# VectorE's loop begun in the middle of a half, and TensorE's 64-row and 64-column products put side by side, in the two local-attention layers of a fused kernel

## The chip, the cores and the metric

One core of one Trainium2 chip runs the whole program in one launch. The metric is the device time of that launch in microseconds, the median of three runs. A profiled execution of the same program gives the trace. Its engines are TensorE (PE, with its weight loads shown as PEld), VectorE (DVE), ScalarE (ACT), GpSimd (POOL) and SyncE (SP, which issues the DMAs).

## What is computed

The program is an RWKV-like block (stages "setup", "mix", "scan", "gate") followed by two layers of windowed attention with a gated MLP (stages "local0", "local1"). The change touches the two local layers alone. For a sequence of 4096 tokens, a batch of 2, 256 channels and 8 heads of 64, each layer computes, all in fp32:

```
h = shift_token(x); q, k, v = split(h @ wqkv)
q = l2norm(q) * qs; k = l2norm(k) * ksc; q, k = rotary_xpos(q, k)
sim = (8 q) @ [k_before, k_own]^T        # a window of 128 queries sees its own and the earlier 128 keys
attn = softmax(mask(sim)); o = attn @ [v_before, v_own]
x = x + o @ wo
h = layernorm(shift_token(x)) * lg + lb
a, g = split(h @ w1 + b1)
x = x + (a * gelu(g)) @ w2 + b2
```

## The kernel before

`local_stage` (line 1409) runs one layer. The tokens of each of the two sequences ("streams" s = 0 and 1) are cut into NW = 32 windows u of 128 tokens. The unit of work is a half, `half(s, u, w)`: the attention of window u of stream s, and, between its pieces, two things for the other stream o: the MLP of its last attended window, and the projection, norm and rotation of q, k and v of its next window. So a layer is 64 halves that alternate between the streams. w is the parity of the window, which picks the buffer.

Every engine has its own written-out order in its own `half`, and semaphores tie them together (`S`, `Q`, `M`, `E` hold them; `.after(n)` is the count to wait for). There is no scheduler. The helper `run` (line 1469) gives all engines the same loop: the first half is written out, then a hardware loop `Fori` of 15 turns with four halves each, then the last halves written out:

```
def body(i, more):
    half(1, 2 * i, 0)
    half(0, 2 * i + 1, 1, more=more)
    half(1, 2 * i + 1, 1, more=more)
    if more:
        half(0, 2 * i + 2, 0)
```

So on every engine the loop's branch stands between the end of one half and the start of the next one.

TensorE's half (line 2106). A half has four head pairs hp. `scores` (line 1997) of one pair are two products of 64 contracted rows, one in the upper and one in the lower 64 rows of the array, into two banks; the profile shows them as `64*128 64x256`, at line 2010. `values` (line 2027) of one pair are products with 64 output columns, `128*64 128x128`, at line 2033. All others use the array whole (`128*128`): `mean` and `variance` of the layer norm (lines 2047, 2053), `project` (line 1976: q, k, v for j = 0, 1, 2), `turn` (line 2024: transposes of the probabilities of a pair), `hidden` (line 2070: three groups of w1), `out` (line 2078: three groups of w2), `turn_q`, `turn_k` (lines 1985, 1993), `project_out` (line 2041), and in layer 1 `turn_out` (line 2086). An fp32 product is executed in two passes, so a `project` is four records, a `hidden` sixteen.

VectorE's half (line 1787). `row_max` (line 1686) adds the mask to the scores of a pair and takes the row maximum (`l_pause` at line 1695 is its first instruction, line 1697 its two main ones, line 1704 the scaled negative maximum `nb`). `inverse_sums` (line 1684) inverts the row sums of a pair. `rotate_q` (lines 1647 to 1649), `sum_q`, `sum_k`, `clamp`, `add_q`, `norm_k` prepare the other stream's q and k. `evacuate` (line 1717) copies the turned probabilities of pairs 1 and 3 to SBUF; ScalarE does pairs 0 and 2. `gate` (line 1751) multiplies the MLP's two halves, one call for each of three groups. `head_out` (line 1711) copies a pair's value product out. `carry` (lines 1725, 1729) copies the last token to the next window and, where w is 0, sets a mask. `attended` (line 1735) adds the residual.

Who waits for whom around the change: `scores` of pair 2 and 3 wait for `row_max` of pair 0 and 1, whose banks they take; `hidden` of group 0 waits for `hn`, which GpSimd makes (line 1591) in its queue behind `normalise` of pair 1 (line 1584), which waits for VectorE's `inverse_sums` of pair 1; `hidden` of group 1 waits for `norm_k`; `out` of group j waits for `gate` of group j; `values` of pair 2 and 3 wait for `head_out` of pair 0 and 1 and for the two `evacuate`s.

Of the kernel before, what the change touches and what calls it, by code (L numbers as in the profile page):

```python
# [1408 lines left out]
def local_stage(nc, persist, a, T, layer):  # L1409
# [5 lines left out]
    NW = T // P  # L1415
    NHP = HEADS // 2
    LAST = layer == 1
# [3 lines left out]
    with ExitStack() as ctx:  # L1421
# [73 lines left out]
        with nc.Block() as block:  # L1495
# [141 lines left out]
            def _(dve):  # L1637
# [69 lines left out]
                def head_out(s, u, hp):  # L1707

                    dve.wait_ge(Q["pv"][s].sem, Q["pv"][s].after(u * NHP + hp))
                    dve.wait_ge(S["wo_ps"][s].sem, S["wo_ps"][s].after(u, 1))  # L1710
                    nc.vector.tensor_copy(oT[s][:, hp], bank[s][OUT[hp % 2]][:, 0:P]).then_inc(Q["oT"][s].sem, 1)
# [72 lines left out]
                    add_q(0, 0)  # L1784
                    norm_k(0, 0)

                def half(s, u, w, mlp=True, more=True):
                    o = 1 - s
                    (um, wm_), (un, wn) = partner(s, u, w)
                    after = s == 0 or more  # L1790
                    row_max(s, u, w, 0)
                    if mlp:
                        deviate(o, um, wm_)
                    row_max(s, u, w, 1)
                    inverse_sums(s, u, 0)
                    if after:
                        rotate_q(o, un, wn)
                    row_max(s, u, w, 2)
                    inverse_sums(s, u, 1)
                    if after:  # L1800
                        sum_q(o, un)
                    row_max(s, u, w, 3)
                    inverse_sums(s, u, 2)
                    if after:
                        sum_k(o, un)
                        clamp(o, un)
                        add_q(o, un)
                    inverse_sums(s, u, 3)
                    if after:
                        norm_k(o, un)  # L1810
                    evacuate(s, u, 1)
                    if mlp:
                        gate(o, um, 0)
                    head_out(s, u, 0)
                    if mlp:
                        gate(o, um, 1)
                    head_out(s, u, 1)
                    carry(s, u, w)
                    if mlp:
                        gate(o, um, 2)  # L1820
                    evacuate(s, u, 3)
                    head_out(s, u, 2)
                    head_out(s, u, 3)
                    if mlp:
                        add_out(o, um, wm_)
                    attended(s, u, w)
                    if mlp and LAST:
                        scale_out(o, um)
# [6 lines left out]
                    if LAST:  # L1835
                        scale_out(s, u)

                run(dve, first, half, last)

            @block.scalar  # L1840
            def _(act):
# [86 lines left out]
                def half(s, u, w, mlp=True, more=True):  # L1928
                    o = 1 - s
                    (um, wm_), (un, wn) = partner(s, u, w)  # L1930
                    after = s == 0 or more
                    act.preload_act_table_set(LN_EXP)
                    exponent(s, u, 0)
                    if mlp:
                        square_dev(o, um)
                    if after:
                        square_q(o, un)
                    exponent(s, u, 1)
                    if mlp:
                        inverse_std(o, um)  # L1940
                    exponent(s, u, 2)
                    if after:
                        square_k(o, un)
                    exponent(s, u, 3)
                    if after:
                        copy_v(o, un, wn)
                        inverse_norms(o, un)
                    evacuate(s, u, 0)
                    if mlp:
                        gelu(o, um, 0)  # L1950
                        gelu(o, um, 1)
                    evacuate(s, u, 2)
                    if mlp:
                        gelu(o, um, 2)
                    if after:
                        copy_qT(o, un)
                        copy_kT(o, un, wn)
# [11 lines left out]
            def _(pe):  # L1969
# [136 lines left out]
                def half(s, u, w, mlp=True, more=True):  # L2106
                    o = 1 - s
                    (um, wm_), (un, wn) = partner(s, u, w)
                    after = s == 0 or more
                    scores(s, u, 0)  # L2110
                    if mlp:
                        mean(o, um, wm_)
                    scores(s, u, 1)
                    if after:
                        project(o, un, wn, 0)
                    scores(s, u, 2)
                    if mlp:
                        variance(o, um)
                    if after:
                        project(o, un, wn, 1)  # L2120
                    scores(s, u, 3)
                    if after:
                        project(o, un, wn, 2)
                    turn(s, u, 0)
                    if mlp:
                        hidden(o, um, 0, after)
                    turn(s, u, 1)
                    values(s, u, 0)
                    if mlp:
                        hidden(o, um, 1, after)  # L2130
                    turn(s, u, 2)
                    values(s, u, 1)
                    if mlp:
                        hidden(o, um, 2, after)
                    turn(s, u, 3)
                    values(s, u, 2)
                    if mlp:
                        out(o, um, 0)
                        out(o, um, 1)
                    values(s, u, 3)  # L2140
# [142 lines left out]
```

## Time and profile before

| what | value |
|---|---|
| median of three runs | 6624.89 us (6621.29 to 6627.57) |
| the profiled execution's own time | 6620.48 us |
| its span, first to last instruction | 6618.7 us |
| PE busy | 5523.2 us, 83% of the span |
| DVE busy | 4142.5 us, 63% |
| ACT busy | 3445.6 us, 52% |
| POOL busy | 2667.4 us, 40% |
| layer 0 (first half to its end) | about 3265 to 4905 us |
| layer 1 | about 4962 to 6617 us |

The shares are averages over stages with different limits. The two local layers fill the second half of the span, and there the page's slices show PE busy for 90% and more in nearly all of them, DVE for about half. "Idle before" in brackets is how long the engine did nothing before that row, and what ended it; "issue" means that nothing the profile shows was waited for. A timeline merges instructions of one line that follow each other; it prints the start of the first and, in the second column, the time from there to the end of the last.

### The profile page before, as it was taken

The page shows a single profiled execution, that of the slowest core. Times are in us where ns is not written, and L with a number is a line of the kernel's source. Part 1 is how long each engine was busy: PE and PEld are TensorE (multiplying, and loading weights), DVE is VectorE, ACT ScalarE, POOL GpSimd, SP SyncE. Part 2 cuts the span into 40 slices and gives each one's busy share as a digit, 9 for nine tenths or more (in the row PEclk, how much of TensorE's full clock was granted, in tenths as well). Part 3 has the DMA queues.
Part 4 walks back from the last instruction along what each step waited for, and adds up shares of the span by engine and source line. Part 5 has one row for each costly group of instructions (what it writes and reads, how often), then busy time and mean ns, then how long its engine had stood idle before and what let it go on. Part 6 is the DMA issues. An engine that isn't in the chain of part 4 may idle for free. (4 is left out here: it accounts for less than half of the span.)

```text
span 6618.7 us, 201409 instructions
## 1 busy us (share of the span) xinstructions
PE 5523.2 (83%) x70816; PEld 4552.2 (69%) x70816; DVE 4142.5 (63%) x13289; ACT 3445.6 (52%) x10441; POOL 2667.4 (40%) x3872
## 2 busy tenths in 40 slices
PE   5555556648888888866599999999979999999999
PEld 4555555548888888854477777777757777777777
DVE  4666666658888989944355555555535555555555
ACT  3555555534444444434355555555535555555555
POOL 1333332236777777720133333333324343333433
PEclk7777777779999999986799999999989999999999
DMA  2222223335565566545200000000010000000000
GB/s 60 62 62 58 61 62 64 64 84 131 129 133 129 130 133 131 130 104 182 93 15 12 14 12 15 12 14 12 15 40 16 19 17 17 20 17 19 17 17 17
DMA packets 999524, 387.22 MB, mean 59 GB/s; under 512 B 775664, under 2 KB 948720, under 8 KB 998512
## 3 DMA queue, kind: packets, MB, share of 16 engines
q1 hardware_dynamic: 998192, 384.78, 24.7%
q14 instruction: 190, 1.56, 0.1%
q8 instruction: 54, 0.88, 0.1%
q10 hardware_dynamic: 1088, 0.00, 0.0%
HBM read 216.32 MB, written 168.30 MB: 58 GB/s over the span
## 5 line engine op out<-in xcount | busy, mean ns | idle before, releaser
L1584 POOL TENSOR_TENSOR l_pn<-l_prob,l_rinv 128x512 f32<-128x512 f32 x512 | 532.2, 1039 | 1430.5 <-DVE l_rinv L1684 1430.1
L1882 ACT ACTIVATE l_prob<-l_prob,l_nb,l_rq 128x256 f32<-128x256 f32 x1024 | 605.0, 592 | 436.7 <-DVE l_nb L1704 359.1
L437 POOL TENSOR_TENSOR cprev<-cum,sg 128x256 f32<-128x256 f32 x64 | 60.4, 962 | 784.2 <-DVE cum L355 784.2
L1171 DVE TENSOR_TENSOR sc_sol<-sc_sol,sc_step 128x15 f32<-128x15 f32 (+7 forms) x960 | 326.6, 340 | 33.0
L1167 DVE TENSOR_TENSOR sc_step<-sc_prob,sc_sol 128x15 f32<-128x15 f32 (+7 forms) x960 | 330.2, 344 | 26.6
L933 POOL TENSOR_TENSOR sc_ax<-sc_late,sc_headmask 128x256 f32<-128x256 f32 x256 | 173.1, 676 | 398.0 <-DMA sc_tok<-scratch_tok 361.0
L1597 POOL TENSOR_TENSOR l_outt<-l_t,l_xat 128x256 f32<-128x256 f32 x64 | 46.4, 726 | 624.8 <-DVE l_t L1766 624.8
L1062 ACT ACTIVATE sc_d_qk<-sc_part,sc_headmask 128x64 f32<-128x64 f32 x1024 | 270.2, 336 | 43.8 <-DMA sc_part<-scratch_part 43.8
L992 PE MATMUL sc_AB<-sc_early,sc_bx 64*64 64x64 f32 x4096 | 176.0, 223 | 125.8 <-POOL sc_kx L933 107.8
L1062 ACT ACTIVATE sc_d_qb<-sc_part,sc_headmask 128x64 f32<-128x64 f32 x1024 | 271.7, 339 | 0.0
L992 PEld LDWEIGHTS sc_AB<-sc_early,sc_bx 64*64 64x64 f32 x4096 | 152.9, 139 | 132.0 <-issue 131.9
L1109 ACT COPY sc_y<-sc_Y 128x64 f32<-128x64 f32 x256 | 54.3, 212 | 359.3 <-PE sc_Y L1000 359.3
L1000 PE MATMUL sc_P<-sc_state,sc_ax 64*64 64x64 f32 x4096 | 174.4, 222 | 79.0 <-issue 63.0
L600 PE MATMUL mxA<-mix,mixw 128*128 128x128 f32 x256 | 70.9, 459 | 203.0 <-DVE mix L373 200.4
L308 DVE TENSOR_TENSOR kk<-mxA,k 128x256 f32<-128x256 f32 x64 | 27.2, 424 | 328.3 <-PE mxA L653 328.3
L954 POOL TENSOR_TENSOR sc_bT<-sc_tok,sc_headmask 128x128 f32<-128x128 f32 x512 | 217.8, 444 | 0.0
L1092 ACT COPY sc_p<-sc_P 128x64 f32<-128x64 f32 x256 | 54.3, 212 | 311.1 <-PE sc_P L1000 311.1
L1000 PEld LDWEIGHTS sc_P<-sc_state,sc_ax 64*64 64x64 f32 x4096 | 148.6, 135 | 97.1 <-issue 94.9
L600 PEld LDWEIGHTS mxA<-mix,mixw 128*128 128x128 f32 x256 | 59.3, 322 | 218.0 <-DVE mix L373 212.8
L674 PE MATMUL mxA<-ident,xn 128*128 128x128 f32 x124 | 34.6, 434 | 200.5 <-DVE xn L351 200.5
L954 POOL TENSOR_TENSOR sc_kT<-sc_tok,sc_headmask 128x128 f32<-128x128 f32 x512 | 201.5, 412 | 0.0
L2078 PE MATMUL l0D<-l_hid,l_w 128*128 128x128 f32 x1536 | 198.8, 279 | 0.0
(383 smaller groups left out, 19049.2 us busy)
## 6 DMA issues: line engine op xcount, KB each, us to landing
scratch_cm<-cm SPq DMA_DIRECT2D x64, 512.0 KB, 4.2
sc_early<-scratch_cm SPq DMA_DIRECT2D x128, 256.0 KB, 3.3
scratch_part<-sc_att SPq DMA_DIRECT2D x64, 512.0 KB, 4.3
sc_part<-scratch_part SPq DMA_DIRECT2D x64, 512.0 KB, 5.2
scratch_tok<-vt SPq DMA_DIRECT2D x512, 48.0 KB, 1.8
l_h<-scratch_h SPq DMA_DIRECT2D x128, 129.0 KB, 2.6
scratch_gr<-gr SPq DMA_DIRECT2D x64, 256.0 KB, 4.1
sc_late<-scratch_cm SPq DMA_DIRECT2D x64, 256.0 KB, 3.9
```

The source lines that it names most:

```text
L437: nc.gpsimd.tensor_tensor(cprev[b][:], cum[b][:], sg[b][:], ALU.subtract).then_inc(S["cprev"][b].sem, 1)
L600: last_ = mm(out, w2(name)[:, kc, m0:m1_], x[:, kc, :], start=(kc == 0), stop=(kc == CC - 1))
L933: return nc.gpsimd.tensor_tensor(dst[:], src.unsqueeze(2).broadcast_to([P, BG, HQ, CH]), headmask[:].unsqueeze(1).unsqueeze(3).broadcast_t ...
L954: last = nc.gpsimd.tensor_tensor(dst[c][:, b * CC:(b + 1) * CC], tok[k][:, c, b, x].unsqueeze(2).broadcast_to([P, CC, HQ, HS]), headmask[: ...
L992: last = mm(bank[at, q * P + x * QH:q * P + (x + 1) * QH], src[c % 2][at, q].rearrange("p h t -> p (h t)"), rhs, start=True, stop=True)
L1000: ins = mm(bank[at, q * P:q * P + QH], lhs[at, q].rearrange("p h t -> p (h t)"), rhs[at, q].unsqueeze(1).broadcast_to([QH, HQ, HS]), start ...
L1062: last = nc.scalar.activation(dst[:, :, h, :], src, ACT.Copy, scale=headmask[:, h:h + 1])
L1167: nc.vector.tensor_tensor(prod, prob[k][:, m:m + 1, m + 1:CH].broadcast_to([P, rows, cols]), x[:, 0:rows, m:m + 1].broadcast_to([P, rows, ...
L1171: ins = nc.vector.tensor_tensor(x[:, 0:rows, m + 1:CH], x[:, 0:rows, m + 1:CH], prod, ALU.add)
L1584: tt(pn[s][:, pair], prob[s][:, pair], rinv[s][:, pair].unsqueeze(2).broadcast_to([P, 2, 2 * P]), ALU.mult).then_inc(Q["pn"][s].sem, 1)
L1882: last_ = nc.scalar.activation(prob[s][:, h], prob[s][:, h], ACT.Exp, scale=rq8[s][:, h:h + 1], bias=nb[s][:, h:h + 1], accum_out=sums[s][ ...
L2078: last_ = mm(bank[s][3][:, c * P:(c + 1) * P], w2[:, m, c * P:(c + 1) * P], hid[s][:, m], start=(c == 0 and m == 0), stop=(c == CC - 1 and ...
```

## The change

VectorE: `half` is cut in two, `scored_part` (up to and including `gate` of group 0) and `valued_part` (the rest). The order of the halves is the same, but the loop's branch now stands between the two parts of a stream-1 half: its `scored_part` ends the body and its `valued_part` begins it. The number of instructions in the loop is the same. Within the half, `rotate_q` and `sum_q` move behind the next `row_max`, `head_out` of pair 0 behind `gate` of group 1, and `gate` of group 2 behind `evacuate` of pair 3.

TensorE: the scores of pairs 0 and 1 follow each other (in layer 1 `mean` still stands between them), as do those of pairs 2 and 3, with `variance` behind them; `turn` of pairs 1 and 2 follow each other, and so do `values` of 0 and 1, and of 2 and 3. ScalarE: `gelu` of group 1 moves behind `evacuate` of pair 2.

```
-                def half(s, u, w, mlp=True, more=True):
+                def scored_part(s, u, w, mlp=True, more=True):
...
                     row_max(s, u, w, 1)
                     inverse_sums(s, u, 0)
+                    row_max(s, u, w, 2)
                     if after:
                         rotate_q(o, un, wn)
-                    row_max(s, u, w, 2)
                     inverse_sums(s, u, 1)
+                    row_max(s, u, w, 3)
                     if after:
                         sum_q(o, un)
-                    row_max(s, u, w, 3)
                     inverse_sums(s, u, 2)
...
                     evacuate(s, u, 1)
                     if mlp:
                         gate(o, um, 0)
-                    head_out(s, u, 0)
+
+                def valued_part(s, u, w, mlp=True, more=True):
+                    o = 1 - s
+                    (um, wm_), _ = partner(s, u, w)
                     if mlp:
                         gate(o, um, 1)
+                    head_out(s, u, 0)
                     head_out(s, u, 1)
                     carry(s, u, w)
+                    evacuate(s, u, 3)
                     if mlp:
                         gate(o, um, 2)
-                    evacuate(s, u, 3)
...
-                run(dve, first, half, last)
+                def half(s, u, w, mlp=True, more=True):
+                    scored_part(s, u, w, mlp, more)
+                    valued_part(s, u, w, mlp, more)
+
+                first()
+                half(0, 0, 0, mlp=False)
+                scored_part(1, 0, 0)
+                with dve.Fori(0, NW // 2 - 1) as i:
+                    valued_part(1, 2 * i, 0)
+                    half(0, 2 * i + 1, 1)
+                    half(1, 2 * i + 1, 1)
+                    half(0, 2 * i + 2, 0)
+                    scored_part(1, 2 * i + 2, 0)
+                valued_part(1, NW - 2, 0)
+                half(0, NW - 1, 1, more=False)
+                half(1, NW - 1, 1, more=False)
+                last(1, NW - 1, 1)
...
                     evacuate(s, u, 0)
                     if mlp:
                         gelu(o, um, 0)
-                        gelu(o, um, 1)
                     evacuate(s, u, 2)
                     if mlp:
+                        gelu(o, um, 1)
                         gelu(o, um, 2)
...
                     scores(s, u, 0)
-                    if mlp:
+                    if mlp and LAST:
                         mean(o, um, wm_)
                     scores(s, u, 1)
+                    if mlp and not LAST:
+                        mean(o, um, wm_)
                     if after:
                         project(o, un, wn, 0)
                     scores(s, u, 2)
+                    scores(s, u, 3)
                     if mlp:
                         variance(o, um)
                     if after:
                         project(o, un, wn, 1)
-                    scores(s, u, 3)
-                    if after:
                         project(o, un, wn, 2)
                     turn(s, u, 0)
                     if mlp:
                         hidden(o, um, 0, after)
                     turn(s, u, 1)
-                    values(s, u, 0)
+                    turn(s, u, 2)
                     if mlp:
                         hidden(o, um, 1, after)
-                    turn(s, u, 2)
+                    values(s, u, 0)
                     values(s, u, 1)
                     if mlp:
                         hidden(o, um, 2, after)
                     turn(s, u, 3)
-                    values(s, u, 2)
                     if mlp:
                         out(o, um, 0)
                         out(o, um, 1)
+                    values(s, u, 2)
                     values(s, u, 3)
```

The loop's branch on VectorE in layer 0, before: `attended`, the branch, and `row_max` of the next half.

```order
L1759 SCALAR_TENSOR_TENSOR l_hout<-l0D,l_lngb,l_x_1 128x128 x2
L1735 TENSOR_TENSOR l_x_0<-l0B,l_h_0 128x2x128
L1481 REGISTER_ALU
L1481 COMPARE_AND_BRANCH
L1695 MEMSET l_pause 128x1
L1697 ISA l_prob,l_mx<-l0B,l_mask_0 128x256
```

The same branch in the changed kernel (its lines are some 20 to 370 higher from there on): it now stands behind `gate` of group 0.

```order
L1717 COPY l_pT<-l0B 128x512
L1748 ISA
L1751 SCALAR_TENSOR_TENSOR l_hid<-l0A,l_b1c,l_gel 128x128 x2
L1849 REGISTER_ALU
L1849 COMPARE_AND_BRANCH
L1751 SCALAR_TENSOR_TENSOR l_hid<-l0B,l_b1c,l_gel 128x128 x2
L1711 COPY l_oT<-l0D 128x128
```

What moved is the branch against the work: the instructions next to it are now two `gate`s.

TensorE in layer 0, before, from the first scores of a half: pairs 0 and 1 (banks B, C and A, D) have `mean` between them, and a `project` follows.

```order
L2010 MATMUL l0B<-l_kT,l_qT 128x256
L2010 MATMUL l0C<-l_kT,l_qT 128x256
L2047 MATMUL l0D<-l_x_0,l_mean_w 128x128 x2
L2005 REGISTER_ALU
L2010 MATMUL l0A<-l_kT,l_qT 128x256
L2010 MATMUL l0D<-l_kT,l_qT 128x256
L1973 ISA
L1976 MATMUL l0A<-l_wqkv,l_h_1 128x512 x2
```

The same place now (scores are line 2030 in the changed kernel, `mean` 2067, `project` 1996):

```order
L2030 MATMUL l0B<-l_kT,l_qT 128x256
L2030 MATMUL l0C<-l_kT,l_qT 128x256
L2025 REGISTER_ALU
L2030 MATMUL l0A<-l_kT,l_qT 128x256
L2030 MATMUL l0D<-l_kT,l_qT 128x256
L2067 MATMUL l0D<-l_x_0,l_mean_w 128x128 x2
L1993 ISA
L1996 MATMUL l0A<-l_wqkv,l_h_1 128x512 x2
```

The four 64-row products are neighbours, and `mean` follows the second pair.

TensorE in layer 0 now, from `turn` of pair 1 on: two `turn`s (line 2044), `hidden` of group 1 (2090), then the value products (2053) of pairs 0 and 1, and `hidden` of group 2. Before, the order was turn, values, hidden, turn, values, hidden.

```order
L2044 MATMUL l0B<-ident,l_pn 128x128 x4
L2036 REGISTER_ALU
L2044 MATMUL l0C<-ident,l_pn 128x128 x4
L2090 MATMUL l0B<-l_hn,l_w 128x128 x8
L2049 ISA
L2050 REGISTER_ALU
L2053 MATMUL l0D<-l_pT,l_V 64x128 x4
L2050 REGISTER_ALU
L2053 MATMUL l0B<-l_pT,l_V 64x128 x4
L2090 MATMUL l0C<-l_hn,l_w 128x128 x8
```

Value products of 64 columns, which stood alone, now stand in pairs.

## Rows read from the trace of the kernel before

**Rows 1.** Four halves, layer 0: busy us (x) of PE, PEld, DVE, ACT, POOL; clock; DMA.
```profile
3284.30:3384.00 99.70, 99.70 (x723) 74.28 (x724) 57.91 (x219) 57.66 (x145) 36.30 (x38) 1.00 0.05 12
```
**Rows 2.** Timeline of PE, layer 0: first scores of halves 2, 31, 32 and 64.
```profile
3284.29 0.48 PE L2010 MATMUL l0B<-l_kT,l_qT 64*128 64x256 f32 x1
...
4024.53 0.48 PE L2010 MATMUL l0B<-l_kT,l_qT 64*128 64x256 f32 x1
...
4049.42 0.48 PE L2010 MATMUL l0B<-l_kT,l_qT 64*128 64x256 f32 x1
...
4865.96 0.48 PE L2010 MATMUL l0B<-l_kT,l_qT 64*128 64x256 f32 x1
```
**Rows 3.** Timeline of PE, layer 1: first scores of halves 3, 4 and 64.
```profile
5007.69 0.48 PE L2010 MATMUL l1B<-l_kT,l_qT 64*128 64x256 f32 x1
...
5032.80 0.48 PE L2010 MATMUL l1B<-l_kT,l_qT 64*128 64x256 f32 x1
...
6577.27 0.48 PE L2010 MATMUL l1B<-l_kT,l_qT 64*128 64x256 f32 x1
```
**Rows 4.** Timeline of DVE behind the loop's branch, in layers 0 and 1.
```profile
4001.01 0.06 DVE L1695 MEMSET l_pause<- 128x1 f32 x1 [3.50 <-issue]
...
5086.41 0.06 DVE L1695 MEMSET l_pause<- 128x1 f32 x1 [2.74 <-issue]
```
**Rows 5.** DMA queues from 3996 to 4005 us: packets, MB, share.
```profile
q14 instruction: 3, 0.02, 0.8%
```
**Rows 6.** Timeline of PE at the same turn of the loop.
```profile
4001.89 0.48 PE L2010 MATMUL l0B<-l_kT,l_qT 64*128 64x256 f32 x1 [1.01 <-DVE l_mx L1697]
...
4003.99 0.71 PE L2053 MATMUL l0D<-l_dsq,l_mean_w 128*128 128x128 f32 x4 [1.41 <-ACT l_dsq L1895]
```
**Rows 7.** A stretch behind another turn, columns as in rows 1.
```profile
3900.00:3904.00 4.00, 3.82 (x8) 1.76 (x8) 3.38 (x15) 3.36 (x11) 1.91 (x2) 0.57 0.00 0
```
**Rows 8.** Timeline of PE in half 31 of layer 0.
```profile
4028.35 0.48 PE L2010 MATMUL l0B<-l_kT,l_qT 64*128 64x256 f32 x1
...
4028.98 0.71 PE L2053 MATMUL l0D<-l_dsq,l_mean_w 128*128 128x128 f32 x4
...
4034.24 1.95 PE L2070 MATMUL l0A<-l_hn,l_w 128*128 128x128 f32 x16
4036.02 0.60 PE L2024 MATMUL l0B<-ident,l_pn 128*128 128x128 f32 x4
4036.55 0.66 PE L2033 MATMUL l0D<-l_pT,l_V 128*64 128x128 f32 x8
4037.14 2.05 PE L2070 MATMUL l0B<-l_hn,l_w 128*128 128x128 f32 x16
4039.03 0.60 PE L2024 MATMUL l0C<-ident,l_pn 128*128 128x128 f32 x4
```
**Rows 9.** Timeline of PE, half 64: last passes of scores of pairs 1 and 2, neighbours.
```profile
4867.55 0.38 PE L2010 MATMUL l0A<-l_kT,l_qT 64*128 64x256 f32 x1
...
4867.98 0.38 PE L2010 MATMUL l0B<-l_kT,l_qT 64*128 64x256 f32 x1
```
**Rows 10.** Timeline of DVE and POOL in half 31 of layer 0.
```profile
4025.51 0.42 DVE L1697 CUSTOM_DVE_ANT_0 l_prob<-l0B,l_mask 128x256 f32<-128x256 f32 x1
...
4029.09 0.69 DVE L1647 TENSOR_TENSOR l_q<-l0A,l_tab 128x512 f32<-128x512 f32 x1 [0.96 <-ACT l_sqq L1845]
...
4032.57 0.73 POOL L1591 TENSOR_TENSOR l_hn<-l_dev,l_rstd 128x256 f32<-128x256 f32 x1
...
4038.00 0.61 DVE L1751 SCALAR_TENSOR_TENSOR l_hid<-l0A,l_b1c,l_gel 128x128 f32<-128x128 f32 x2 [0.65 <-ACT l_gel L1909]
...
4039.89 0.61 DVE L1751 SCALAR_TENSOR_TENSOR l_hid<-l0B,l_b1c,l_gel 128x128 f32<-128x128 f32 x2 [1.08 <-ACT l_gel L1909]
...
4040.61 0.54 DVE L1725 COPY l_x<-l_x 128x2 f32<-128x2 f32 x1
...
4043.42 0.68 DVE L1717 COPY l_pT<-l0A 128x512 f32<-128x512 f32 x1
```

More of the change, by code:

```diff
@@ L1785, in first, with scored_part @@
                     norm_k(0, 0)
-                def half(s, u, w, mlp=True, more=True):
+                def scored_part(s, u, w, mlp=True, more=True):
                     o = 1 - s
@@ L1795, in half @@
                     inverse_sums(s, u, 0)
+                    row_max(s, u, w, 2)
                     if after:
                         rotate_q(o, un, wn)
-                    row_max(s, u, w, 2)
                     inverse_sums(s, u, 1)
+                    row_max(s, u, w, 3)
                     if after:
                         sum_q(o, un)
-                    row_max(s, u, w, 3)
                     inverse_sums(s, u, 2)
@@ L1813, in half, with valued_part @@
                         gate(o, um, 0)
-                    head_out(s, u, 0)
+                def valued_part(s, u, w, mlp=True, more=True):
+                    o = 1 - s
+                    (um, wm_), _ = partner(s, u, w)
                     if mlp:
                         gate(o, um, 1)
+                    head_out(s, u, 0)
                     head_out(s, u, 1)
                     carry(s, u, w)
+                    evacuate(s, u, 3)
                     if mlp:
                         gate(o, um, 2)
-                    evacuate(s, u, 3)
                     head_out(s, u, 2)
@@ L1836, in last, with half @@
                         scale_out(s, u)
-                run(dve, first, half, last)
+                def half(s, u, w, mlp=True, more=True):
+                    scored_part(s, u, w, mlp, more)
+                    valued_part(s, u, w, mlp, more)
+                first()
+                half(0, 0, 0, mlp=False)
+                scored_part(1, 0, 0)
+                with dve.Fori(0, NW // 2 - 1) as i:
+                    valued_part(1, 2 * i, 0)
+                    half(0, 2 * i + 1, 1)
+                    half(1, 2 * i + 1, 1)
+                    half(0, 2 * i + 2, 0)
+                    scored_part(1, 2 * i + 2, 0)
+                valued_part(1, NW - 2, 0)
+                half(0, NW - 1, 1, more=False)
+                half(1, NW - 1, 1, more=False)
+                last(1, NW - 1, 1)
             @block.scalar
@@ L1950, in half @@
                         gelu(o, um, 0)
-                        gelu(o, um, 1)
                     evacuate(s, u, 2)
                     if mlp:
+                        gelu(o, um, 1)
                         gelu(o, um, 2)
@@ L2110, in half @@
                     scores(s, u, 0)
-                    if mlp:
+                    if mlp and LAST:
                         mean(o, um, wm_)
                     scores(s, u, 1)
+                    if mlp and not LAST:
+                        mean(o, um, wm_)
                     if after:
@@ L2116, in half @@
                     scores(s, u, 2)
+                    scores(s, u, 3)
                     if mlp:
@@ L2120, in half @@
                         project(o, un, wn, 1)
-                    scores(s, u, 3)
-                    if after:
                         project(o, un, wn, 2)
@@ L2127, in half @@
                     turn(s, u, 1)
-                    values(s, u, 0)
+                    turn(s, u, 2)
                     if mlp:
                         hidden(o, um, 1, after)
-                    turn(s, u, 2)
+                    values(s, u, 0)
                     values(s, u, 1)
@@ L2135, in half @@
                     turn(s, u, 3)
-                    values(s, u, 2)
                     if mlp:
@@ L2139, in half @@
                         out(o, um, 1)
+                    values(s, u, 2)
                     values(s, u, 3)
```

## The prediction

> **What bounds the kernel now.** I read the two local layers by stage, first by the busy times of a stretch. In four halves of layer 0 TensorE is busy for 99.70 of 99.70 us at full clock, VectorE and ScalarE for 58, GpSimd for 36 [rows 1]. So inside a half TensorE is the bound, and only what shortens its own stream, or stops it from waiting, can shorten the layer. Then its timeline, at the first scores of successive halves. A half takes 4049.42 - 4024.53 = 24.89 us in layer 0 [rows 2] and 25.11 us in layer 1 [rows 3]. From half 2 to half 64 lie 62 halves: 1581.67 us, against 62 x 24.89 = 1543.18, so 38.5 us are not the halves' own. From half 3 to half 64 of layer 1 it is 1569.58 - 61 x 25.11 = 37.9 us. Together 76.4 us. Every other half has the plain length: the excess sits in one half of four, where the loop turns (14 turns in each layer that jump back, 2.7 us each on average).
>
> At a turn VectorE does nothing for 3.50 us in layer 0 and 2.74 us in layer 1 before the first instruction of the body, with no wait that the profile knows ("issue") [rows 4]. Three packets of instructions, 0.02 MB, arrive just then [rows 5]. So I read the gap as VectorE waiting for its next instructions behind the branch. TensorE then waits 1.01 us for the row maximum and 1.41 us for the square of the deviation, which waits for VectorE too [rows 6]. Behind some turns the granted clock falls as well (0.57 over 4 us [rows 7], so most of that stretch at 1.2 instead of 2.4 GHz). ScalarE, GpSimd and TensorE have the same loop but show no such gap.
>
> **What a change of array shape costs.** The reader is to compare the starts of neighbouring rows on TensorE [rows 8]. A `hidden` of 16 whole-array passes takes 4036.02 - 4034.24 = 1.78 us between whole-array products, so four passes take 0.44. The four passes of a `turn` in front of the 64-column products take 0.53: 0.09 to leave a shape. A `hidden` behind them takes 1.89: 0.11 to come back. For scores, one visit takes 0.63 us [rows 8], while the second of two neighbours takes 0.43 from last pass to last pass [rows 9]: 0.20 of the visit goes to entering and leaving. So joining two visits of scores saves 0.20 + 0.09 + 0.11 = 0.40. The value products take 0.59; a pass of 128 columns is half of the 0.215 that rows 9 give for 256, so their four pairs of passes are worth 0.43, and 0.16 is for entering and leaving. Joined, they save 0.16 + 0.09 + 0.11 = 0.36.
>
> **The change, part by part.** *Scores.* Layer 0 joins pairs 0 and 1 and pairs 2 and 3: 0.80 a half. Layer 1 keeps `mean` between 0 and 1: 0.40. *Value products.* Both layers join two times: 0.72. Neighbouring value products that don't wait are not in the trace; the bounds are nothing saved (if each visit paid for its own weights) and 0.36 each. I take 0.36, because the scores, the nearest rows, show the full saving. That makes 1.52 us a half in layer 0 and 1.12 in layer 1: halves of 23.37 and 23.99. Over 62 halves each that have both partners: 94.2 + 69.4 = 164. The first and last half of a layer wait for other engines in between; for them I take 1 us in all, between 0 and 4.
>
> The Trainium skill, "TensorE: Matmul & The Clock Gate", section "Step-by-step: what each phase is for", says that weight loads are pulled ahead of running products where their rows don't conflict or they go to the background buffer. By that rule coming into a new shape would cost nothing and only leaving it would be saved: the sum would be some 80 us smaller. Against it speaks the 0.11 by which `hidden` is longer behind a change of shape [rows 8].
>
> *Does TensorE stay the bound?* Its waits have to end earlier by what its stream gains. Counted from the first scores of a half, `hidden` of group 0 starts at 4034.24 - 4024.53 = 9.71 now [rows 2, 8] and would start at 8.91. It needs `hn`, which starts at 8.04 and ends at 8.77 now [rows 10]. The chain to it is the same work in another order: `rotate_q`, `row_max` of pair 2, `inverse_sums`, `normalise`, then `hn`: 8.04 - 4.56 = 3.48 us from the start of `rotate_q` to that of `hn`. Today it begins at 4.56, when the square of q is done. In the changed order it begins with `row_max` of pair 2, 0.98 us behind its scores (4025.51 against 4024.53), and these start at 3.42 (3.82 now, less 0.40): 4.40. `hn` then ends at 4.40 + 3.48 + 0.73 = 8.61, 0.30 before it is needed. In layer 1 both move alike. That is the thinnest of the steady waits by my count; `norm_k` before `hidden` of group 1, and the row maxima before pairs 2 and 3 and before `turn`, have about half a microsecond or more. I cost them at nothing; each 0.1 us by which `hn` is later than those 0.30 costs 12.4 us over 124 halves.
>
> *The turn of the loop.* The branch now stands behind `gate` of group 0. Its fetch is no shorter; it must be hidden. That gate starts at 13.47 now [rows 10], and at about 12.7 when the half has gained 0.8 by then. It ends at 13.3; 3.5 us idle make the next gate start at 16.8 and end at 17.4. TensorE wants it for `out` of group 1 at about 17.7. From the start of that gate to the end of `carry` it is 1.26 us [rows 10], and I allow 0.2 for the mask copy, so `evacuate` of pair 3 runs from 18.3 to 18.95; `values` of pair 3 wants it at 19.2. So 3.5 us just fit, and the 2.74 of layer 1 fit with 0.8 to spare. Late next in layer 0 is that `evacuate`: each 0.1 us beyond costs 1.4 us over 14 turns. I leave 2 us for it. With no wait of TensorE left, the falls of the clock go too: the whole 76.4 us. The other moves (`head_out`, `gelu` of group 1, `sum_q`) stand in front of nothing that TensorE takes within a microsecond. No DMA changes its place in a queue.
>
> *Sum.* 164 + 1 + 76 - 2 = 239 us. The profiled execution took 6620.5 us, so 6381.5; the median of the runs shown lies 4.4 above it, so **6386 us**.
>
> The Trainium skill, "Runtime: NRT & Kernel Launch", section "Instruction fetch mechanics", gives most engines room for 512 instructions and says that a taken branch stalls when its target has left that window. VectorE's body of 380 might fit in it. If it did, the gap of rows 4 would be a wait that the profile doesn't know, and could come back at another place: the third rival. The packets of rows 5 speak against it.
>
> **Rivals.**
> *Waits take part of it.* `hn` or `norm_k` come later than worked out, for instance because ScalarE's exponents of pair 1 stand in front. At 0.5 us a half beyond the room, 62 us are lost: 6448. For it: only 0.30 us of room, where there are 0.94 today. Against: the engines other than TensorE are idle for 42% and more [rows 1].
> *The value products save nothing side by side.* Less 0.72 x 124 = 89: 6475. Against it are rows 9, for the other shape.
> *The turn is not hidden*, because the gap is no fetch, or grows, or another engine's branch shows once VectorE's is gone: 76 back, 6462.
> *Slower than before.* One mechanism: VectorE takes `row_max` of pair 2 in front of `rotate_q`, so its whole queue, `hn` on GpSimd behind it, and `hidden` of group 0 wait for the second pair of scores. It decides against the change once `hidden` of group 0 waits for more than 239 / 124 = 1.93 us in each half, that is once `hn` ends at 10.84 instead of 8.61. At 2.5 us of waiting, 124 x 2.5 = 310 are lost: 6696. The chain is 3.48 us in either order, so this needs an error of 2.2 us.
>
> **How the numbers follow.** Forecast, 0.70; waits take part, 0.14; value products save nothing, 0.05; turn not hidden, 0.08; slower, 0.02; both gains met by waits of the same size, 0.01. The forecast's own range: down to 6370 if the changes of shape save 7% more and the ends of the layers 4 us; up to 6405 if `hn` is late by 0.1 and the turns of layer 0 show 0.3. The range for 8 in 10 reaches into the first rival, to 6435. A measurement of this kernel can tell about 0.2% from no change, 13 us: faster 0.97, the same 0.01, slower 0.02.
>
> **What would show it.** In the profile after: 23.4 and 24.0 us between first scores of halves; no idle of TensorE at the turns; VectorE's "issue" gap of some 3 us in front of the second `gate`; neighbouring scores 0.43 apart, neighbouring value products too; the granted clock at 1.00 throughout a layer. Halves longer than 23.6 and 24.2, with idle time in front of `hidden`, would show the first rival; a gap of TensorE in front of `out` or of the last `values` in one half of four the third. A time above 6435 would make the forecast wrong, and so would one below 6370, which would mean that a change of shape costs more than the rows give.

## The result and the profile after

The changed kernel takes **6385.76 us** (median of 4 runs, 6383.9 to 6394.36), the kernel before 6626.23 (median of 4, 6621.29 to 6634.49): a ratio of 0.9638, with a 95% interval of 0.9622 to 0.9655. The forecast was 6386. The profiled execution took 6383.90 us with a span of 6382.1, so against the profiled execution of before (6620.5) 236.6 us are gone. The stages ahead of the local layers move their start by several us from execution to execution (layer 0's first scores start at 3265.5 us before, at 3266.9 after, and between 3264.8 and 3282.0 in the experiments), so lengths of halves tell more than a difference of medians.

The first view is again TensorE's timeline, at the first scores of halves. Layer 0: half 2, the half of the turn with its two neighbours (three starts), and half 64. They answer to [rows 2].

```profile
3286.73 0.48 PE L2030 MATMUL l0B<-l_kT,l_qT 64*128 64x256 f32 x1
...
4012.34 0.48 PE L2030 MATMUL l0B<-l_kT,l_qT 64*128 64x256 f32 x1
...
4035.74 0.48 PE L2030 MATMUL l0B<-l_kT,l_qT 64*128 64x256 f32 x1
...
4059.15 0.48 PE L2030 MATMUL l0B<-l_kT,l_qT 64*128 64x256 f32 x1
...
4737.94 0.48 PE L2030 MATMUL l0B<-l_kT,l_qT 64*128 64x256 f32 x1
```

Layer 1: two successive halves and half 64, against [rows 3].

```profile
5213.54 0.48 PE L2030 MATMUL l1B<-l_kT,l_qT 64*128 64x256 f32 x1
...
5237.56 0.48 PE L2030 MATMUL l1B<-l_kT,l_qT 64*128 64x256 f32 x1
...
6342.52 0.48 PE L2030 MATMUL l1B<-l_kT,l_qT 64*128 64x256 f32 x1
```

A half takes 23.40 to 23.41 us in layer 0, and the half in which VectorE's loop turns (from 4035.74) takes 23.41 like the others. From half 2 to half 64 it is 4737.94 - 3286.73 = 1451.2 us = 62 x 23.41: no excess is left, where there were 38.5 us. In layer 1 a half takes 24.02, and here too the 62 from half 2 (4853.23) to half 64 are equal.

The busy times over all these halves at once (columns as in [rows 1]) show TensorE without a gap and at full clock in both layers; the falls behind a turn [rows 7] are gone.

```profile
3286.70:4738.10 1451.40, 1451.40 (x11163) 1162.82 (x11164) 924.60 (x3380) 891.10 (x2233) 561.61 (x588) 1.00 0.06 14
4853.20:6342.50 1489.30, 1489.30 (x11285) 1172.45 (x11284) 944.35 (x3441) 897.62 (x2233) 606.13 (x649) 1.00 0.07 19
```

VectorE's gap is still there, at its new place. Its timeline at the turn of the half from 4035.74: the first `gate`, the gap, the second `gate`, and `evacuate` of pair 3, which TensorE takes next. Against [rows 4].

```profile
4048.66 0.61 DVE L1751 SCALAR_TENSOR_TENSOR l_hid<-l0A,l_b1c,l_gel 128x128 f32<-128x128 f32 x2 [0.70 <-ACT l_gel L1929]
4051.80 0.61 DVE L1751 SCALAR_TENSOR_TENSOR l_hid<-l0B,l_b1c,l_gel 128x128 f32<-128x128 f32 x2 [2.54 <-issue]
...
4052.93 0.68 DVE L1717 COPY l_pT<-l0A 128x512 f32<-128x512 f32 x1
```

The DMA queues from 4045 to 4054 us, and VectorE's waits from 3300 to 6330 us (engine, line, releaser: us in total, times, longest):

```profile
q14 instruction: 2, 0.02, 0.7%
```

```profile
DVE l_hid L1751 <- issue: 72.3, 28, 2.9
```

The gap comes 28 times, 2.58 us each on average and 2.9 at most, and packets of instructions arrive as before [rows 5], but two at each of the 28 turns, where three came at each turn of layer 0 before. It is 0.6 to 1.0 shorter than the 3.50 of [rows 4]. `evacuate` of pair 3 starts 4052.93 - 4035.74 = 17.19 us into the half; in a half without a turn it is 16.99 (4005.93, in the half that starts at 3988.94). TensorE wants it at 19.16, so VectorE catches up in time.

### The profile page after: what moved, and what is told of

Same layout as the page of the kernel before. It is cut to its first block and busy times, and to the rows that moved or that the text cites. A ratio compares the mean times of both kernels' runs of the same rounds, so it can differ in the third digit from the quotient of the medians.

```text
span 6382.1 us, 201409 instructions
## 1 busy us (share of the span) xinstructions
PE 5354.2 (84%) x70816; PEld 4583.3 (72%) x70816; DVE 4196.0 (66%) x13289; ACT 3451.7 (54%) x10441; POOL 2668.3 (42%) x3872
```

## Experiments

Ten further kernels; each is compared with the kernel before on its own chip (medians 6625.7 to 6631.7 there). Lengths of halves come from the starts of their first scores, as above.

### The turn and the orders apart

*turn_only* keeps the orders of before on all engines and takes only the new shape of VectorE's loop. *order_only* is the change with the old loop:

```
-                first()
-                half(0, 0, 0, mlp=False)
-                scored_part(1, 0, 0)
-                with dve.Fori(0, NW // 2 - 1) as i:
...
-                last(1, NW - 1, 1)
+                run(dve, first, half, last)
```

> The kernel before with one edit: VectorE's loop begins behind the first gate; every order is as before. Theory (the terms are independent, the turn of the loop costs what TensorE waited for at it): halves keep their 24.89 and 25.11 us, all of them, the excess of 76 us goes: 6626 - 76 = 6550, perhaps 3 to 6 more where evacuate of pair 3, which here stands behind gate of group 2, comes late in the half of the turn. Rival (the gap is a wait that comes back elsewhere): 6600 to 6626, with a gap on TensorE in one half of four.

> The changed kernel with VectorE's loop begun between two halves, as before; all new orders kept. Theory (terms add up): halves of 23.41 and 24.02 us, and at each turn TensorE waits some 2.5 us for the row maximum and the square of the deviation as before: 6386 + 76 = 6462. Rival (a shorter half leaves less room, so a turn costs more, at least 1 us each for 28 turns): 6490 or more.

**turn_only: 6550.47 us** (ratio 0.9883, 0.9866 to 0.9899). Every half takes 24.89 in layer 0 and 25.11 in layer 1, those of the turn too. The gap stands in front of the copy behind the first value product, 28 times and 72.2 us in all, again 2.58 each, and no half gets longer by it. One of them, in VectorE's timeline of this kernel:

```profile
4003.41 0.29 DVE L1711 COPY l_oT<-l0D 128x128 f32<-128x128 f32 x1 [2.55 <-issue]
```

**order_only: 6465.57 us** (ratio 0.9751, 0.9735 to 0.9768). The plain halves are 23.41 and 24.02, exactly those of the changed kernel, but the halves of the turn are longer: by 57.8 us in all over 14 of layer 0 and by 25.3 over 14 of layer 1, 83 us together where the kernel before lost 76. TensorE's waits from 3300 to 6400 us (here the scores are L2018, `variance` L2061):

```profile
PE l0A L2018 <- DVE l_mx L1697: 22.8, 15, 1.8
PE l0B L2018 <- DVE l_mx L1697: 15.7, 14, 1.3
PE l1A L2018 <- DVE l_mx L1697: 11.9, 14, 0.8
PE l1B L2018 <- DVE l_mx L1697: 6.9, 14, 0.7
...
PE l0D L2061 <- ACT l_dsq L1903: 1.0, 1, 1.0
```

Now the row maxima of both pairs are late, one wait behind the other, and the wait of `variance` for the square is gone (it was 21.7 + 19.7 us before): with the pairs of scores together, `variance` comes after both waits and finds its square ready. In TensorE's timeline of one turn and, behind it, the busy times of the stretch that follows:

```profile
3386.39 0.48 PE L2018 MATMUL l0B<-l_kT,l_qT 64*128 64x256 f32 x1 [1.19 <-DVE l_mx L1697]
...
3388.57 0.48 PE L2018 MATMUL l0A<-l_kT,l_qT 64*128 64x256 f32 x1 [1.48 <-DVE l_mx L1697]
```

```profile
3388.60:3392.60 4.00, 4.00 (x12) 2.12 (x13) 3.81 (x19) 3.30 (x11) 2.09 (x3) 0.64 0.00 0
```

The granted clock is 0.64 over these 4 us: a fall of 3.4 us, of which 2.9 lie in this stretch, to 1.2 in place of 2.4 GHz. That happened at 9 of 14 turns in layer 0 and at 1 in layer 1, against 3 and 3 before. A turn with a fall costs 4.6 to 5.0 us in layer 0, one without 2.8 to 3.1.

In layer 0 a turn of *order_only* without a fall is thus dearer by some 0.6 us than before (2.2 to 2.8 there), and six more turns have a fall; in layer 1 the turns are cheaper, 25.3 us in all against 37.9.

So the two parts are worth 77 us (the turn, on the old orders: 6627.6 - 6550.5) and 162 us (the orders, with the old loop: 6627.6 - 6465.6), and the turn is worth 80 on the new orders. The parts add up to within 3 us of the whole.

### Is the loop the whole of the excess?

In *before_no_loop* and *after_no_loop* VectorE's program is written out, with no branch at all. Everything else is that of before, and of the change. The line that does it in *after_no_loop*:

```
-                with dve.Fori(0, NW // 2 - 1) as i:
+                for i in range(NW // 2 - 1):
```

> The kernel before with VectorE's loop written out (no branch; all orders as before, the other engines keep their loops). Theory (the gap is the fetch of instructions behind a taken branch, and straight code is fetched ahead in time): no gap, halves of 24.89 and 25.11 us throughout, 6626 - 76 = 6550, as in the run with the turned loop alone. Rival (the gap belongs to the first row_max of a stream-1 half of even window, a wait that the profile doesn't know, or straight code is fetched too slowly): 6626 or more, with gaps left.

> The changed kernel with VectorE's loop written out. Theory (the turned loop hides its fetch wholly): nothing is left to gain, 6386, halves of 23.41 and 24.02. Rival (some of the turn still costs time): a few us to 20 us faster.

**before_no_loop: 6548.56 us** (0.9887, 0.9871 to 0.9904); **after_no_loop: 6385.3 us** (0.9637, 0.9621 to 0.9653). Halves of 24.89 and 25.11, and of 23.41 and 24.02, all equal to 0.01, and no gap of VectorE that comes once in a turn. The first shows that VectorE's loop alone made the 76 us. The second shows that the changed kernel has nothing more to gain there: its branch already costs nothing that can be measured. And it speaks against the rival in which another engine's branch shows once VectorE's is hidden: with no branch on VectorE nothing new appears.

The Trainium skill, "Runtime: NRT & Kernel Launch", section "Instruction fetch mechanics", says that instructions are prefetched in sequence only and that a taken branch whose target isn't at hand stalls for a fetch. The trace agrees: whole layers of straight code without such a gap, 2.5 to 3.6 us at each branch that is taken. The same section gives most engines room for 512 instructions, in two pages; VectorE's body of 380 is smaller and still stalled at all 28 turns, so being smaller than that room did not help it here.

### Scores and value products apart

*scores_only* is the change with the value products taken one at a time, as before (on VectorE and ScalarE the orders that go with them too). *values_only* is the change with the old order of scores (and of VectorE's scored part). From TensorE's program, the first piece *scores_only*, the second *values_only*:

```
                     turn(s, u, 1)
-                    turn(s, u, 2)
+                    values(s, u, 0)
                     if mlp:
                         hidden(o, um, 1, after)
-                    values(s, u, 0)
+                    turn(s, u, 2)
                     values(s, u, 1)
...
                     scores(s, u, 2)
-                    scores(s, u, 3)
                     if mlp:
                         variance(o, um)
                     if after:
                         project(o, un, wn, 1)
+                    scores(s, u, 3)
```

> The changed kernel with the value products, gates, head copies and gelu in their old order; scores in pairs and loop turned. Theory (joining two visits of value products saves 0.36 us, twice a half, 124 halves): halves of 24.13 and 24.74, 6386 + 89 = 6475. Rival (all of the shorter half came from the scores, or from waits): 6386 to 6400.

> The changed kernel with mean, variance, project and scores, and VectorE's scored part, in their old order; value products in pairs and loop turned. Theory (joining two visits of scores saves 0.40 us, twice a half in layer 0 and once in layer 1): halves of 24.21 and 24.42, 6386 + 50 + 25 = 6461. Rival as for the run with scores alone: close to 6386.

| kernel | median us | ratio (95%) | half, layer 0 | half, layer 1 |
|---|---|---|---|---|
| turn_only | 6550.47 | 0.9883 (0.9866 to 0.9899) | 24.89 | 25.11 |
| scores_only | 6483.1 | 0.9781 (0.9764 to 0.9797) | 24.10 | 24.71 |
| values_only | 6461.46 | 0.9747 (0.973 to 0.9763) | 24.20 | 24.42 |
| the change | 6385.76 | 0.9638 (0.9622 to 0.9655) | 23.41 | 24.02 |

The scores give 24.89 - 24.10 = 0.79 in layer 0, where two pairs are joined, and 25.11 - 24.71 = 0.40 in layer 1, where one is: 0.395 a join. The value products give 0.69 in either layer (24.89 - 24.20, 25.11 - 24.42), so 0.345 a join. Both together give 1.48 and 1.09, which is the sum to the hundredth. The median of *scores_only* is 8 us above what was expected; its layer 0 began at 3275.8 us in the profiled execution, 9 later than the changed kernel's, and its halves are right, so that is not from the local layers.

The rows of the changed kernel in one half show where the saving sits. Neighbouring visits of value products, with the `hidden` on either side:

```profile
4000.50 1.95 PE L2090 MATMUL l0B<-l_hn,l_w 128*128 128x128 f32 x16
4002.38 0.66 PE L2053 MATMUL l0D<-l_pT,l_V 128*64 128x128 f32 x8
4002.87 0.61 PE L2053 MATMUL l0B<-l_pT,l_V 128*64 128x128 f32 x8
4003.40 2.05 PE L2090 MATMUL l0C<-l_hn,l_w 128*128 128x128 f32 x16
4005.29 0.60 PE L2044 MATMUL l0A<-ident,l_pn 128*128 128x128 f32 x4
```

The first visit takes 0.49, the second 0.53 with leaving the shape in it; `hidden` in front of them takes 1.88 (it too pays for leaving, 0.10), the one behind 1.89. The visit alone took 0.59 [rows 8].

The Trainium skill, "TensorEngine Tiling (Array Packing)", section "Key Properties", says that changing the tiling mode drains TensorE, with no price. By these runs a pair of changes, in and out, costs 0.395 us around scores and 0.345 around value products.

### How much room has `hn`?

GpSimd computes the product for `hn` once more (and in *hn_thrice* twice more) into a spare tile, ahead of the real one:

```
+                    tt(spare0[s][:], dev[s][:], rstd[s][:].unsqueeze(1).broadcast_to([P, CC, P]), ALU.mult)
                     tt(hn[s][:], dev[s][:], rstd[s][:].unsqueeze(1).broadcast_to([P, CC, P]), ALU.mult).then_inc(S["hn"][s].sem, 1)
```

> The changed kernel with one more product of the same shape on GpSimd in front of hn (into a tile that nobody reads), in each half: hn comes 0.69 us later. In the profile after, hn ends 0.50 us before hidden of group 0 starts, some 0.46 before it is needed. Theory (that is the thinnest wait, and each us beyond it costs a us of the half): TensorE waits 0.23 us a half for hn, halves of 23.64 and 24.25, 6386 + 28 = 6414. Rival (something absorbs it, or the room is wider): 6386. Rival (another wait behind hn gives way first, at turn of pair 2 or 3): over 6440.

> The same with two more products: hn comes 1.38 us later. Theory: TensorE waits 0.92 us a half, halves of 24.33 and 24.94, 6386 + 114 = 6500. The difference to the run with one more is 124 x 0.69 = 86, the slope of one for one. Rival (absorbed in part): under 6470.

**hn_twice: 6464.51 us** (0.9752, 0.9736 to 0.9768); **hn_thrice: 6548.34 us** (0.9879, 0.9862 to 0.9895). From the one to the other it is 84 us, 0.68 for each of 124 halves, as long as one such instruction: the slope was expected. The level was not: *hn_twice* lies 79 us above the change where 28 were expected. Its halves take 23.75 to 23.98 and 24.37 to 24.60, on average 0.52 more, which is 64 us (its layer 0 also began 13 us later than the changed kernel's, in the profiled execution). First the changed kernel in the half that starts at 3988.94, one of stream 1: `hn` on GpSimd, `row_max` of pair 2 on VectorE, and TensorE's `hidden` of group 0 with the row behind it.

```profile
3996.61 0.73 POOL L1591 TENSOR_TENSOR l_hn<-l_dev,l_rstd 128x256 f32<-128x256 f32 x1
```

```profile
3993.11 0.42 DVE L1697 CUSTOM_DVE_ANT_0 l_prob<-l0B,l_mask 128x256 f32<-128x256 f32 x1 [0.95 <-issue]
```

```profile
3997.84 1.95 PE L2090 MATMUL l0A<-l_hn,l_w 128*128 128x128 f32 x16
3999.63 0.60 PE L2044 MATMUL l0B<-ident,l_pn 128*128 128x128 f32 x4
```

The same kernel in the next half, which starts at 4012.34 and is one of stream 0: GpSimd and VectorE.

```profile
4020.24 0.74 POOL L1591 TENSOR_TENSOR l_hn<-l_dev,l_rstd 128x256 f32<-128x256 f32 x1
```

```profile
4016.74 0.42 DVE L1697 CUSTOM_DVE_ANT_0 l_prob<-l0B,l_mask 128x256 f32<-128x256 f32 x1
```

Then *hn_twice*, in a half of stream 0 that starts at 3993.60, with its scores of pair 2 at 3.42: GpSimd, VectorE and TensorE.

```profile
4001.50 0.73 POOL L1592 TENSOR_TENSOR l_spare<-l_dev,l_rstd 128x256 f32<-128x256 f32 x1
4002.19 0.73 POOL L1593 TENSOR_TENSOR l_hn<-l_dev,l_rstd 128x256 f32<-128x256 f32 x1
```

```profile
3998.00 0.42 DVE L1699 CUSTOM_DVE_ANT_0 l_prob<-l0B,l_mask 128x256 f32<-128x256 f32 x1
```

```profile
4002.97 2.05 PE L2092 MATMUL l0A<-l_hn,l_w 128*128 128x128 f32 x16 [0.30 <-POOL l_hn L1593]
```

In the changed kernel `hn` ends at 3996.61 + 0.73 - 3988.94 = 8.40 in the half of stream 1, and `hidden` starts at 8.90: room of 0.50. In the half of stream 0 it ends at 4020.24 + 0.74 - 4012.34 = 8.64, against the same 8.90: room of 0.27. There `row_max` of pair 2 starts 4.40 into the half in place of 4.17, 0.98 behind its scores in place of 0.76, and all that follows is later by as much. It is so throughout both layers: in the halves of stream 0 the room is 0.27 (in all that lie inside VectorE's loop), in those of stream 1 it is 0.41 to 0.50. The expectation took the 0.50 of one half for all.

In *hn_twice*, in a half of stream 0, `hn` ends at 4002.19 + 0.73 - 3993.60 = 9.32. That is 0.68 later than in the like half of the changed kernel, as much as the added instruction takes, so the chain ahead of it has not moved. What the half loses is the excess over the room, 0.69 - 0.27 = 0.42, plus two parts that come with any such wait: `hidden` starts 0.05 behind the end of `hn` (4002.97 against 4002.92), and it is itself 0.10 longer, 4004.86 - 4002.97 = 1.89 (the next row starts at 4004.86) where it takes 3999.63 - 3997.84 = 1.79 without a wait. Together 0.57, and the half takes 23.98 in place of 23.41. Halves of stream 1 in layer 0, with more room, lose 0.43 and 0.51 in turn: the first is again the excess and 0.15, while in the second kind, one half of four, `hidden` starts 0.24 behind the end of `hn`, which stays open. So the expected level failed in two terms: the room, which is 0.27 in every second half, and the price of having a wait at all, 0.15 us and in one half of four about 0.34. The difference between *hn_twice* and *hn_thrice* can't show this price, since both pay it.

Why VectorE takes up the second pair of scores later in the halves of stream 0 is not settled. It goes with VectorE's loop: in *after_no_loop*, where its program has no loop, the distance is 0.76 in the halves of either stream, and `hn` has room of 0.50 or more in nearly all of them.

### What can still be had in layer 1

*mean_behind* joins pairs 0 and 1 of scores in layer 1 too, as layer 0 has it:

```
-                    if mlp and LAST:
-                        mean(o, um, wm_)
                     scores(s, u, 1)
-                    if mlp and not LAST:
+                    if mlp:
                         mean(o, um, wm_)
```

*turn_out_inside* has that too and puts `turn_out` between the two output halves of `project_out` (`turn_out` in the loop over m), with `scale_out` ahead of `attended` on VectorE:

```
                     for m in range(CC):
+                        if m == 1 and between:
+                            between()
...
-                    project_out(s, u)
-                    if mlp and LAST:
-                        turn_out(o, um)
+                    project_out(s, u, (lambda: turn_out(o, um)) if mlp and LAST else None)
```

> The changed kernel with mean behind the second pair of scores in layer 1 too, so that pairs 0 and 1 are neighbours there. The scores of pair 1 take a bank that VectorE's last step of the half before (scale_out) still reads; before the change that step ended 0.64 us behind the start of the half, and the second scores would now start at 0.43. Theory (0.40 saved for a joined visit, 0.2 to 0.25 given back to that wait): halves of layer 1 0.15 to 0.2 shorter, 9 to 12 us, 6375. Rival (the wait eats it, which is why mean stands there): 6386 or slower.

> The same, and in layer 1 turn_out stands in the middle of project_out on TensorE and scale_out ahead of attended on VectorE, so that the bank is free before the half begins. Theory: the whole 0.40 us a half of layer 1, halves of 23.62, 62 x 0.40 = 25 us, 6361. Rival (attended comes later by scale_out's 0.36 and mean waits, or turn_out waits for add_out in the middle of project_out): 6375 to 6395.

**mean_behind: 6382.08 us** (0.9626, 0.9612 to 0.9639). Halves of layer 1 take 23.89: 0.13 less, 8 us over the layer, where a join is worth 0.40. In TensorE's timeline of this kernel the second pair starts late:

```profile
5242.03 0.38 PE L2106 MATMUL l1D<-ident,l_hout 128*128 128x128 f32 x2
5242.34 0.48 PE L2030 MATMUL l1B<-l_kT,l_qT 64*128 64x256 f32 x1
...
5242.67 0.38 PE L2030 MATMUL l1C<-l_kT,l_qT 64*128 64x256 f32 x1
5243.04 0.48 PE L2030 MATMUL l1A<-l_kT,l_qT 64*128 64x256 f32 x1
```

VectorE's timeline at the same place has `scale_out`, which reads l1D:

```profile
5242.57 0.41 DVE L1766 TENSOR_TENSOR l_t<-l1D,rows 128x256 f32<-128x256 f32 x1
```

`turn_out` writes l1D just ahead of the scores, `scale_out` reads it until 5242.98, and the second pair (l1A, l1D) starts 0.06 after that, 0.37 behind the first pair's last pass instead of 0.21. Its own first passes then take 0.32 instead of 0.21. So 0.16 + 0.11 = 0.27 of the 0.40 are given back, and 0.13 are left, as measured. TensorE's row names no wait there, but among those that waited for `scale_out` the trace has the weight load of these scores, 62 times. The expectation had this wait right, and the next kernel, where `scale_out` ends before the half begins, shows the whole saving. Half 2 of *mean_behind* itself, ahead of which no `scale_out` runs, takes 23.63. **turn_out_inside: 6365.91 us** (0.9606, 0.9593 to 0.9619), with halves of 23.62 in layer 1, the whole 0.40:

```profile
5395.24 0.38 PE L2108 MATMUL l1D<-ident,l_hout 128*128 128x128 f32 x2
5395.46 1.06 PE L2063 MATMUL l1B<-l_oT,l_wo 128*128 128x128 f32 x8
5396.44 0.48 PE L2030 MATMUL l1B<-l_kT,l_qT 64*128 64x256 f32 x1
...
5396.77 0.38 PE L2030 MATMUL l1C<-l_kT,l_qT 64*128 64x256 f32 x1
5396.98 0.38 PE L2030 MATMUL l1A<-l_kT,l_qT 64*128 64x256 f32 x1
```

This version beats both kernels: 20 us under the change (25 from the halves), and the intervals of the two ratios don't meet. Layer 1 is still 0.21 a half above layer 0, about what `turn_out`'s two passes take (5395.46 - 5395.24 = 0.22).

## Why the prediction was right

*The bound.* It held that a half is TensorE's stream and nothing else. Shown: no waits of TensorE in the halves, 1451.40 busy of 1451.40.

*Scores, 0.40 a join.* Measured 0.395 in layer 0 and 0.40 in layer 1, with the value products apart or joined. Entering plus leaving plus the slower product behind [rows 8, 9] was the right sum.

*Value products, 0.36 a join.* Measured 0.345. The transfer from rows of another shape held within 5%; it rested on taking a pass of 128 columns as half of one of 256. The rival in which they save nothing side by side is out: *values_only* against *turn_only*.

*Halves.* 23.37 and 23.99 forecast, 23.41 and 24.02 measured, 0.03 to 0.04 a half too hopeful: 62 x 1.48 + 62 x 1.09 = 159 us instead of 164. That is the value products' 0.03 and the scores' 0.01. The further 1 us for first and last halves is small beside what moves there for other reasons. The two first halves take 1.1 us more after than before (18.81 and 19.87 against 19.81 and 19.99), but hardly more in *after_no_loop* than in *before_no_loop* (19.90 and 19.97 against 19.86 and 19.98). From the first scores of half 64 to the next layer, or to the end, it is 96.65 and 41.4 us before and 95.30 and 39.6 after, 3.2 us less. Together 2.1 us less, inside the 0 to 4 that were allowed; how much of it is the change is not shown.

*The turn, 76.4 us, less 2.* All of it came back, and *before_no_loop* shows that it was the branch's. The 2 us held back for `evacuate` of pair 3 weren't needed. The step was mis-sized on the safe side: the gap was taken as 3.5 us, as in [rows 4], and measured 2.54 there, so the second `gate` started at 16.06 into the half where 16.8 was worked out, and `evacuate` at 17.2 instead of 18.3.

These sum to 159.3 + 76.4 = 235.7 us; with the 2.1 of the ends, less 1.4 by which layer 0 began later, it is the 236.6 measured on the profiled executions to 0.2. The forecast had 239: the two small errors (164 for 159, and 2 held back) partly cancel. It was 2.4 us off for the profiled execution (6381.5 against 6383.9). That it hit the median within 1 us is luck: it added 4.4 us for the distance of the median to the profiled execution, as before, and this time the distance was 1.9.

*`hn`, the thinnest wait.* By the rows its end was to be at 8.61, with 0.30 to spare. In the halves of stream 0, the kind that [rows 10] come from, it ended at 8.64 with 0.27, so the chain was right to 0.03; in those of stream 1 it ended at 8.40 to 8.50, since `row_max` of pair 2 starts 0.76 behind its scores there and not 0.98. The note beside it (each 0.1 us beyond the room costs 12.4 us) is right as a slope, 84 us from *hn_twice* to *hn_thrice* for 0.69 us more, but it left out what having such a wait adds, on average 0.2 us a half or some 24 us. *hn_twice*, 0.39 beyond the predicted room, would have lost 48 us by the note, and its halves lost 64. The rival in which waits take part of the gain was mostly one of a longer chain, which did not come: TensorE had no such wait in the change.

*Slower than before.* It wanted `hn` at 10.84. *hn_thrice*, with 1.38 us more on GpSimd's path, is still 1.2% faster than before.

## What to carry over

Where one engine's stream is the bound, price a reordering by differences between starts of neighbouring rows, with the shape of what stands on either side: it gave each join within 5%. A loop's branch belongs at the place where its engine has the longest time until the next result is wanted: the gap is still there (2.5 to 2.9 us here) and costs nothing. And before you call a wait harmless because it has room, read the room in every kind of half that the loop has, and lengthen its chain by a known amount once: the room was 0.50 us in the half that was read and 0.27 in the next one, and a wait, once there, cost at least 0.15 us more than its excess.

## What was not expected of the hardware

- The same gap behind a branch differs with its place in the program, for the same number of instructions in the body. With the branch between two halves (*order_only*) it is 3.1 to 3.4 us plus a second one of 0.5 to 0.8 in layer 0, and 2.7 to 3.0 in layer 1; in the middle of a half (the change, *turn_only*) it is 2.5 to 2.9 in both layers. The packets of instructions go with it: three follow the branch at each of the 14 turns of layer 0 with the second gap, two at every other turn, 2.4 to 3.1 us from one to the next. Where a program has no loop on VectorE they come some 35 us apart. What decides between two and three stays open.
- In layer 0 a tighter order made the hidden cost larger: with the branch at its old place the turns cost 57.8 us instead of 38.5. The granted clock fell to 1.2 GHz at 9 of 14 turns instead of 3, and the turns without a fall were longer too. TensorE's two waits at a turn were 1.0 to 1.3 and 1.5 to 1.8 us there; before, 0.5 to 1.2 and 1.41.
- What TensorE does first after a wait was itself longer at both places looked at: `hidden` takes 1.89 us instead of 1.79, as much as behind a change of shape, and in *mean_behind* the first passes of the late scores take 0.32 instead of 0.21.
- In the changed kernel and its variants with a loop on VectorE, this engine takes up the second pair of scores 0.98 us after they start in the halves of stream 0 inside the loop, and 0.76 after in those of stream 1; without the loop it is 0.76 in all. Why is not settled.
